# Four cross attentions on one core: more groups whose mask is applied as a product on GpSimd, other turns of VectorE and GpSimd, other orders of steps

## The reference, cut to what matters

```python
q, k, v = norm(x) @ Wq + bq, ctx @ Wk + bk, ctx @ Wv + bv      # 16 heads
logits = einsum('bhqd,bhkd->bhqk', q, k) / 4
# first attention:  logits += (1 - mask) * -1e9; attn = softmax(logits) * group_prob
# second attention: logits = where(mask == 0, -1e9, logits); attn = softmax(logits)
# third and fourth: attn = softmax(logits)
x = x + einsum('bhqk,bhkd->bhqd', attn, v) @ Wo + bo
```

## Time and profile before

| | us |
|---|---|
| runs of the kernel | 1538.9, 1538.91, 1542.71; median 1538.91 |
| the profiled execution, its own time | 1537.95 |
| its span | 1536.7 |
| TensorE busy | 1420.2 (92% of the span) |
| VectorE busy | 980.9 |
| ScalarE busy | 760.1 |
| GpSimd busy | 526.1 |

### The profile page before, as it was taken

One profiled execution on the slowest core, in us unless ns is written; L12 is line 12 of the kernel. 1 busy time (PEld: TensorE's weight loads), 2 busy tenths in 40 slices (PEclk: granted clock), 3 DMA queues, 4 the chain that ended last, 5 costly groups with the idle time before them and its releaser, 6 DMA issues. The chain is left out here.

```text
span 1536.7 us, 29870 instructions
## 1 busy us (share of the span) xinstructions
PE 1420.2 (92%) x11216; PEld 838.7 (55%) x11216; DVE 980.9 (64%) x2274; ACT 760.1 (49%) x1020; POOL 526.1 (34%) x638
## 2 busy tenths in 40 slices
PE   8999997999999998799999888699999896999987
PEld 3765753555555555545555555335555583555555
DVE  4444445888888863587878334288886235888842
ACT  5144140444444433168888733247777221777762
POOL 4565242566666650365555522011111001011100
PEclk9999997999999997889999999989999998999999
DMA  8888994244444308235567074536668521476800
GB/s 269 272 273 258 283 287 147 42 67 66 66 65 66 104 2 124 52 49 87 84 94 172 1 195 117 173 63 110 102 100 224 85 39 45 80 108 94 159 8 7
DMA packets 131657, 178.21 MB, mean 116 GB/s; under 512 B 14365, under 2 KB 105525, under 8 KB 124342
## 3 DMA queue, kind: packets, MB, share of 16 engines
q1 hardware_dynamic: 117610, 160.90, 49.2%
q10 hardware_dynamic: 13904, 15.41, 3.1%
HBM read 132.44 MB, written 43.78 MB: 115 GB/s over the span
## 5 line engine op out<-in xcount | busy, mean ns | idle before, releaser
L894 ACT ACTIVATE prob_a<-ps 128x1024 f32<-128x1024 f32 x464 | 456.2, 1023 | 268.1 <-PE ps L768 170.7
L907 DVE CUSTOM_DVE_ANT_0 dump_a<-ps,neg_q 128x512 bf16<-128x512 f32 (+1 forms) x485 | 329.8, 718 | 89.2 <-PE ps L748 87.2
L748 PE MATMUL ps<-kop,qop 116*128 116x512 bf16 x1024 | 343.8, 405 | 38.0 <-DMA qop<-qparts 22.7
L911 DVE TENSOR_REDUCE best_a<-ps 128x1 f32<-128x512 f32 (+1 forms) x488 | 318.6, 709 | 48.5 <-PE ps L748 48.0
L765 PE MATMUL ps<-qop,kop 116*128 116x256 bf16 x2048 | 343.8, 274 | 3.2 <-ACT prob_a L894 2.6
L765 PEld LDWEIGHTS ps<-qop,kop 116*128 116x128 bf16 x2048 | 194.5, 98 | 128.0 <-ACT prob_a L894 12.9
L792 PE MATMUL ps<-prob_a,vop_a 128*32 128x256 f32 x3072 | 191.7, 383 | 3.1 <-POOL prob_a L1026 2.2
L748 PEld LDWEIGHTS ps<-kop,qop 116*128 116x128 bf16 x1024 | 90.1, 102 | 177.2 <-issue 79.5
L1007 POOL TENSOR_TENSOR used_a<-prob_a,gT 128x1024 f32<-128x1024 f32 x64 | 151.6, 2368 | 87.4 <-DVE used_a L924 67.3
L768 PE MATMUL ps<-neg_k,identb 128*128 128x512 bf16 x416 | 159.0, 382 | 0.0
L986 POOL CAST mpart_a<-nmax_a 128x2 bf16<-128x2 f32 x64 | 25.3, 396 | 369.4 <-DVE nmax_a L916 369.4
(11 more groups left out here) (318 smaller groups left out, 1511.7 us busy)
## 6 DMA issues: line engine op xcount, KB each, us to landing
kop<-kparts SPq DMA_DIRECT2D x448, 128.0 KB, 5.0
kparts<-kp SPq DMA_DIRECT2D x64, 384.0 KB, 4.7
vals<-vst SPq DMA_DIRECT2D x16, 1024.0 KB, 6.9
vraw<-vals SPq DMA_DIRECT2D x64, 256.0 KB, 6.4
e_w<-in_e_w SPq DMA_DIRECT2D x4, 2048.0 KB, 11.4
z_w<-in_z_w SPq DMA_DIRECT2D x24, 256.0 KB, 6.9
ctxT<-in_ctxT SPq DMA_DIRECT2D x8, 512.0 KB, 7.8
raw<-in_mask ACTq DMA_DIRECT2D x16, 256.0 KB, 5.7
```

Of the source, the lines that this page charges most:

```text
L748: return pe.matmul(out, qop[0:R_ALL, h, t * P:(t + 1) * P], kop[0:R_ALL, h % UNROLL, j * CHUNK:(j + 1) * CHUNK], start=True, stop=True)
L894: act.activation(prob[:, n % NP, :], st_bank(n), ACT.Exp).then_inc(S("exp_done"), 1)
L907: dve.tensor_tensor_reduce(out=dump[:, k % 2, 0:width], in0=bank, in1=c.neg_q[:, t, j * CHUNK:j * CHUNK + width], scale=1.0, scalar=-3.0e3 ...
L911: dve.tensor_reduce(out, bank, AX.X, ALU.max).then_inc(sem, 1)
```

## The change

- `SHIELDS`: the first attention gets two shielded groups (3 and 7), where it had none; the second has four (1, 3, 5, 7) where it had three (2, 5, 7).
- In the first attention VectorE weighs the even groups and GpSimd the odd ones (before, the other way round). VectorE's weights are steps **W** of the order string. GpSimd weighs a group once VectorE has weighed all lower ones, and after its own shield product where there is one.
- In the first attention the row sums of a shielded group wait for the shield product.
- The masks are summed and compared in the first attention, during the scores in advance (in four parts behind the double steps 2 to 5), and GpSimd changes groups 3 and 7 there; in the second attention only groups 1 and 5 are changed. The second attention's query stage has the usual filling matmuls in place of the sum.
- New order strings for all three kinds; AHEAD 24 in place of 30 (weighted) and 22 in place of 24 (others); `SUM_AT, TURN_AT` (2, 3) in place of (1, 2), and (3, 5) in place of (2, 5) in the second attention.

The diff at its core:

```diff
-SHIELDED = 1
+SHIELDS = [(3, 7), (1, 3, 5, 7), (), ()]
...
-WEIGHTED_ORDER = "CCK KCCV CCKT KCCFV CCK KCCV CCK KCCV".replace(" ", "")
-MASKED_ORDER = "CCK CCK CCK CVV CCK KCCKF CKCT KCCC VV".replace(" ", "")
-PLAIN_ORDER = "CCKCKCCV CCKCKCV CKCCT KF CKCCKC VV".replace(" ", "")
+WEIGHTED_ORDER = "W CCCK CCK CCK C V W CCK CK T CCK W V C W F CK CK VV".replace(" ", "")
+MASKED_ORDER = "CCK CK CCCK K CCC VV CK CK F CCK CTK CC VV".replace(" ", "")
+PLAIN_ORDER = "CCK CK CC V CCK CK CC V K CK CF CK CTK CC VV".replace(" ", "")
...
-        if l == SHIELDED:
-            dve.wait_ge(S("masks_summed"), 1)
-            dve.tensor_scalar(blind[:, :], c.ps[:, 7, 0:NT], (KEYS - 0.5) * NEG, None, ALU.is_le).then_inc(S("blind_found"), 1)
...
-        if l == SHIELDED:
-            for k in range(KT):
-                ins = pe.matmul(c.ps[:, 7, 0:NT], c.idle[:, 0:P], c.neg_k[:, k, :], start=(k == 0), stop=(k == KT - 1))
-            ins.then_inc(S("masks_summed"), 1)
-        else:
-            keep_warm(c, pe, NORM_FILL)
+        keep_warm(c, pe, NORM_FILL)
...
-    AHEAD = 30 if weighted else 24
+    AHEAD = 24 if weighted else 22
...
-    SUM_AT, TURN_AT = (1, 2) if weighted else (2, 5) if by_query else (3, 5)
-    SHIELD = (2, 5, 7) if l == SHIELDED else ()
-    SHARED = (0, 2, 4, 6) if weighted else ()
+    SUM_AT, TURN_AT = (2, 3) if weighted else (3, 5)
+    SHIELD, COUNT_AT = SHIELDS[l], (2, 3, 4, 5)
+    SHARED = (1, 3, 5, 7) if weighted else ()
...
         def sums(n):
 
             g = n % NGROUP
-            pe.wait_ge(S("exp_done"), n + 1)
+            if g in SHIELD:
+                pe.wait_ge(S("shielded"), shields(n) + 1)
+            else:
+                pe.wait_ge(S("exp_done"), n + 1)
...
+            if l == 0 and n in COUNT_AT:
+                for k in range(KT // 4 * COUNT_AT.index(n), KT // 4 * (COUNT_AT.index(n) + 1)):
+                    ins = pe.matmul(sums_out, c.idle[:, 0:P], c.neg_k[:, k, :], start=(k == 0), stop=(k == KT - 1))
+                ins.then_inc(S("masks_summed"), 1)
             if n == SC // 2 + 2:
+                if l == 0:
+                    pe.wait_ge(S("blind_found"), 1)
                 turn_max(0)
...
+            if l == 0 and n == SC // 2:
+                dve.wait_ge(S("masks_summed"), len(COUNT_AT))
+                dve.tensor_scalar(c.blind[:, :], sums_out, (KEYS - 0.5) * NEG, None, ALU.is_le).then_inc(S("blind_found"), 1)
...
-                    n = NGROUP * h + (at - AHEAD - SC * h) // 2 - 2
-                    if weighted and (at - AHEAD) % 2 == 0 and n >= 0 and n % NGROUP in own:
-                        weigh(n)
+                elif step == "W":
+                    k = weighs.next()
+                    if k > 0:
+                        weigh(NGROUP * ((k - 1) // len(own)) + own[(k - 1) % len(own)])
...
-            if n > 0:
-                pool.wait_ge(S("weighted"), n // 2)
+            pool.wait_ge(S("weighted"), len(own) * h + len([k for k in own if k < g]))
+            if g in SHIELD:
+                pool.wait_ge(S("shielded"), shields(n) + 1)
...
+        fresh = [g for g in SHIELD if l == 0 or g not in SHIELDS[l - 1]]
...
-        if l == SHIELDED:
-            pool.wait_ge(asked.S("blind_found"), 1)
-            for i, g in enumerate(SHIELD):
+        if l > 0:
+            for i, g in enumerate(fresh):
                 find_seen(i, g)
         split(0)
         fill(1)
+        if l == 0:
+            pool.wait_ge(S("blind_found"), 1)
+            for i, g in enumerate(fresh):
+                find_seen(i, g)
...
+            if weighted:
+                if h + 1 < H:
+                    split(h + 1)
+                for i, g in enumerate(SHARED):
+                    if g in SHIELD:
+                        shield(h, g)
+                    weigh(h, g)
+                    if i == 0 and 0 < h < H - 1:
+                        fill(h + 1)
+            else:
+                for g in SHIELD[:2]:
+                    shield(h, g)
+                if h + 1 < H:
+                    split(h + 1)
+                if 0 < h < H - 1:
+                    fill(h + 1)
+                for g in SHIELD[2:]:
+                    shield(h, g)
```

26 lines of the change are left out of this document (6 added, 20 removed).

## The result

The changed kernel takes 1578.55 us (median of four runs, 1575.70 to 1582.41), the kernel before 1540.81 beside it (four runs, 1538.90 to 1545.24). The ratio is 1.0235 with a 95% interval of 1.0211 to 1.026: slower, by more than the 1564.5 that was forecast, and inside the range of 1548 to 1586. The profiled execution took 1576.07 (span 1574.8), 38.1 more than that of before; the forecast's sum was +25.6.

What follows compares the result with a forecast made beforehand. The prediction took TensorE as the bound before and the GpSimd-VectorE chain as the first attention's bound after. Terms +32.3 - 5.3 - 1.4 = +25.6 on the profiled 1537.95 gave 1563.6, with 1.0 for the median 1564.5 us; range 1548 to 1586.

Steps and rivals of the forecast that it cites:

- The shared chain becomes the bound of the first attention: First attention: GpSimd and VectorE work that never overlaps outlasts TensorE's 17.95 us a head and sets the head.
- Rival (b): First attention: GpSimd's mask products do not keep VectorE out, TensorE's 17.95 bounds long heads, total 1523.6; chance 0.08.
- Rival (a): First attention: GpSimd keeps its turn between ready operations, 22.3 us a head, total 1594; chance 0.17, with other longer chains.
- Rival (c): Whole kernel: the gains cancel, needing a first-attention head of about 18.7 or a free start and short heads; chance 0.05.
- A head of 20.15: First attention: one head takes 20.15 us, 1.3 more than now, bounds 19.2 and 22.3.
- The walked order: First attention: GpSimd and VectorE operations followed in turn from one end of weight 5 to the next, 20.15 us.
- The start and the last heads: First attention: GpSimd free at 278.7, head 1 begins at 292.2; head 15 takes 18.0, last read of sums at 598.7.
- 19.96 of work of which no two pieces overlap: First attention, one head: weight pairs 14.32, mask products 4.14, split 0.93 and copy 0.57 sum to 19.96 us.
- the other waits fit: First attention: exponential 3 ends at about 10.4, wanted at 11.0; exponential 7 ends while VectorE's 6 runs; no added time.
- The second attention, -5.3: Second attention: heads of 13.15 for 13.57 us and smaller terms give -5.3 us in all (-8 to 0).
- GpSimd has four products ...: hidden: Second attention: GpSimd's four products, 8.3 + 1.5 of 13 us, have no VectorE weights beside them and cost nothing.
- Plain attentions, -1.4: Third and fourth attentions: no change a head; in advance -1.14, later +0.43, so -0.7 each, -1.4.

Runs made afterwards that it cites:

- run 3: Changed kernel with VectorE's weight in the first attention reading one SBUF input, group probabilities left out on even groups: 1552.8 us.
- run 1: Changed kernel with no shielded group in the first attention, everything else kept: 1549.63 us, ratio to the kernel before 1.0061.
- run 5: Changed kernel with only group 3 shielded in the first attention, bias and query weights later, second attention's split and tile changes moved: 1567.09 us.
- run 6: Changed kernel with only group 7 shielded in the first attention, bias and query weights later, second attention's split and tile changes moved: 1551.09 us.
- Runs 9 to 11: Changed kernel with 28 scores in advance for 24 (1578.84 us); also group 3 alone and second-attention edits (1565.2); also VectorE's weight 0 behind five reads (1563.23).
- run 4: Changed kernel with the second attention's split behind the first mask product and mask tiles changed after the query parts: 1570.01 us, ratio to before 1.0197.
- run 8: Changed kernel with eighteen matmuls of no effect filling TensorE's waits at the end of the first attention: 1578.96 us.

## Why the prediction was right, and where it was not

**The shared chain becomes the bound of the first attention: right, and it is the exclusion.** TensorE's busy time there is under its period for the first time, and run 3, with the same lengths of work but one input on VectorE, takes 1.7 us a head off. Rival (b), 1523.6, fell with it. By its own sign it would have held, for the records of a mask product and a weight do overlap by up to 1.17 us. But such a pair never takes less than 3.21 together, the 2.13 and 1.08 of one behind the other, and L924's mean went to 1918 ns. Rival (a), 22.3 a head, fell by the 3.11 and the 1.20 above: a waiting VectorE gets the turn between two ready GpSimd operations. Where that rival had placed its loss, at the end of weight 5, exponential 7 was not ready (it ends at 490.98, weight 5 at 490.39), as the forecast had said. Rival (c) would have wanted a head of 18.7; that is what the order gives without mask products (run 1), not with them.

**A head of 20.15: measured 19.81.** The walked order is good to 0.34; VectorE's weights 2 and 4 came in each one operation earlier than I had them, and weights 3 and 5 ran back to back. 0.34 x 14 = 4.8 us explain why the first attention ended at 594.5 and not at 598.7: +28.1 for +32.3. The start and the last heads were sized right: by the forecast's own marks, the ends of weight 5, head 0 comes at 292.25 for 292.2, head 15 takes 18.16 for 18.0, and from there to the last read it is 6.8 for 6.4.

**"19.96 of work of which no two pieces overlap. So the shared chain becomes the bound": wrong as a reason.** That sum came within 0.2 of the walked order by chance. With product 7 away it is 17.9, and the head stays at 19.82 (run 5); with product 3 away the head is 18.49 (run 6). What sets the head is a loop in which product 3, VectorE's weights and GpSimd's weights 3 and 5 have a part and which from the end of weight 5 to product 3 goes by two ways of nearly one length: VectorE's weight 6, its eight reads, the maximum, the split, weight 1 and the copy; and TensorE's values 5, eight scores and three groups of key products, values 6 and 7, exponential 2, the read of sums and exponential 3. In the kernel after the first is the longer by some 0.8 us: GpSimd comes to product 3 at 481.63, and exponential 3 had ended at 480.8. The walk had the first way right; of the second it said "the other waits fit", and it does fit, with nothing to spare. Runs 9 to 11 show the second come out as soon as the first is shortened: product 3 then starts some 0.7 earlier after weight 5, but the turns of VectorE behind it cost 0.55 more, and 0.10 to 0.16 us a head is left.

**The second attention, -5.3: measured +6.8.** This is the step that failed. It is 12.1 us of the 12.5 between +25.6 and +38.1; the plain attentions bring 4.5 more, and the first took 4.2 less. Its heads were to take 13.15 and took 13.65. The term "GpSimd has four products ...: hidden" did not hold, because the split stands behind the second of them. With the split moved it is 13.34 (run 4): the exchange of matmuls for passes gives 0.23 a head where I had put 0.42, for a cause that no run looked for. Reckoned from the first exponentials of heads 1 and 14, which the new place of the read does not move, the +6.8 are these: 3.5 from the last read of the first attention to the first scores (85.78 for 82.29), 1.6 from there to head 1 (29.94 for 28.33), 1.1 in thirteen heads, and 0.7 from head 14 to the last read, where I had put +1.3.

Of the 3.5, two query parts held up by a change of a mask tile are 1.6 (2.58 for the pair that took 0.99 before, gone in run 4), a term that the forecast put at nothing. The fold at the lower clock would be 2.1, but run 8 took it away and its first scores came no earlier (85.59), so it can't be added. That stretch took 79.8 to 87.7 in the changed kernels, and the rest of the 3.5 stays open. The 1.6 between the first scores and head 1 went with the split, too: 28.53 in run 4.

**Plain attentions, -1.4: measured +3.1.** From the first scores to the last read each takes what it took: 199.32 for 199.38 in the third, 199.28 for 199.29 in the fourth. A head takes 11.69 for 11.65, 0.5 in an attention, where I had no change. Two scores fewer in advance gave 0.3 us and not 1.1 (first scores to key products 13.62 for 13.92, in the second attention 13.82 for 14.14): TensorE's last scores wait for the same reads either way. The third attention's loss stands ahead of it, in a stretch that the change does not touch (121.56 for 118.25). It took 118.3 to 124.4 in all the kernels, so 3 us there can be what one execution differs from another. But the two lowest are the two kernels with unchanged plain attentions, so a part of it may be the change's after all; no run settles that.

**The range and the chances.** The measured median lies in the range by the room that was given to rival (a), which was not what happened: it lies just above the forecast's own range of 1550 to 1577, by costs of the second attention and of stretches between. Of what I had named as showing the prediction wrong one thing came, a second attention at over 13.57, though by GpSimd's order and not by ScalarE's waits. No kernel tested beats the kernel before; the nearest is the second attention alone, 1546.2 for 1540.4.

## What to carry to other kernels

Before work is moved to a less busy engine, look whether its operations and those of a neighbour ever overlap in the trace, and walk the order of both through one period. A sum of work that can't overlap is a lower bound and no model: take one piece out and see whether the period moves, since two equal products can cost 1.3 us and nothing. And walk a second way through the same period to its end, and the small operations queued behind the moved one too: here a split of 0.9 us behind a product cost 0.31 us a head, more than the 0.23 that the exchange of matmuls for products gave. Last, ask of every mark by which a time is measured whether the edit has moved it.

## What the runs showed of the hardware

- VectorE, waiting, gets the turn between two GpSimd operations that are issued back to back; the second is recorded with the wait in it, at the three places looked at: 3.11 for a product of 2.13, 1.20 for one of 0.22, 2.25 for an addition of 1.27. So such a record's start is not the start of its work.
- A VectorE operation of 1024 float32 columns with one input took 1.22 us, 64 times of 64, though 48 of these ran beside a GpSimd product (run 3); one with two inputs, 1.22 at its shortest, had a mean of 1.92 in the kernel after, and together with a GpSimd product that its record overlaps it never took less than the two one behind the other.
- Even small work is shut out: two query parts, 0.99 together before the change, took 2.58 behind a change of a mask tile.
- Within two waits of TensorE, 1.99 and 1.50 us, at the end of an attention that ran at a granted clock of 1.00, the clock fell to 0.50 and stayed there to 599; it cost 2.1 us in a chain of short matmuls, and with the waits filled it did not happen.
